# A graph-network layer on one core: GpSimd's record scatters made to wait, four by four, for the four in front

## The reference, cut to what matters

```python
h = jnp.maximum(_layernorm(x), 0.0)
xn = layernorm(h) * ln_w + ln_b
w_phys = (silu(rbf @ w1 + b1) @ w2 + b2) * cutoff[:, None]      # one row of 256 per edge
msg_phys = xn[col] * w_phys
scores = sum(Q[row] * K[col]) / sqrt(HD) * cutoff               # 8 heads
combined = msg_phys + gate * softmax(scores) * V[col]
aggr = segment_sum(combined, row, num_segments=n)
out = x + h + aggr @ wo + bo
```

## Time and profile before

| what | us |
|---|---|
| median of 3 runs | 5735.35 (5733.4 to 5738.21) |
| profiled execution, first to last instruction (its span) | 6164.1 |
| of it before the first scatter of filter rows starts | 157.8 |
| first scatter to the end of the last | 2841.3 |
| barrier, then `edges` from | 3003.07 |
| `finish`, its products from | 6049.9 to the end at 6164.1 |

### The profile page before, as it was taken

One profiled execution on the slowest core, in us unless ns is written; L12 is line 12 of the kernel. 1 busy time (PEld: TensorE's weight loads), 2 busy tenths in 40 slices (PEclk: granted clock), 3 DMA queues, 4 the chain that ended last, 5 costly groups with the idle time before them and its releaser, 6 DMA issues. The chain is left out here.

```text
span 6164.1 us, 116650 instructions
## 1 busy us (share of the span) xinstructions
PE 5392.7 (87%) x24352; PEld 3865.5 (63%) x24353; DVE 4459.1 (72%) x7861; ACT 3179.5 (52%) x10634; POOL 3908.3 (63%) x3475
## 2 busy tenths in 40 slices
PE   3778988888888988988589999999999999999999
PEld 3555655555555655655466666666666666666667
DVE  8888866555544444422389999899899999999995
ACT  4445555455555545544355555555555555555553
POOL 1666766666666666656567776667676777776671
PEclk9999999999999999999799999999999999999999
DMA  5233334333334434333599999999999999999965
GB/s 182 92 111 131 114 136 136 116 133 134 119 130 138 138 105 144 132 105 131 199 307 299 307 304 302 304 303 303 300 306 303 305 305 304 301 305 302 309 209 173
DMA packets 584375, 1306.07 MB, mean 212 GB/s; under 512 B 81230, under 2 KB 384118, under 8 KB 582945
## 3 DMA queue, kind: packets, MB, share of 16 engines
q0 software_dynamic: 221536, 881.08, 41.0%
q1 hardware_dynamic: 311780, 345.48, 18.7%
q10 hardware_dynamic: 50850, 77.03, 3.5%
HBM read 1024.15 MB, written 324.38 MB: 219 GB/s over the span
## 5 line engine op out<-in xcount | busy, mean ns | idle before, releaser
L1023 POOL DMA_INDIRECT ukvx<-kvx_table,udst x1760 | 2096.2, 1191 | 936.9 <-issue 503.1
L337 POOL DMA_INDIRECT records<-rows,slot_i x1660 | 1744.8, 1051 | 1096.8 <-ACT rows L825 589.0
L692 PE MATMUL w_ps<-w2s,hid 128*128 128x256 f32 x6656 | 1617.8, 397 | 196.1 <-DVE rows L606 167.3
L692 PEld LDWEIGHTS w_ps<-w2s,hid 128*128 128x128 f32 x6656 | 1277.6, 197 | 564.7 <-issue 210.3
L606 DVE TENSOR_TENSOR rows<-w_ps,b2b 128x512 f32<-128x512 f32 x832 | 569.4, 687 | 1104.3 <-PE w_ps L692 607.5
L806 ACT ACTIVATE hid<-hid_ps,b1t 128x512 f32<-128x512 f32 x832 | 525.4, 682 | 1227.6 <-remote 523.3
L1132 PE MATMUL ag_ps<-ukvx,uonehot 128*128 128x256 f32 x3520 | 1006.6, 405 | 155.8 <-issue 76.6
L1112 PE MATMUL uq_ps<-aggr,uonehotT 128*128 x3520 | 975.4, 400 | 1.8 <-issue 1.8
L1135 PE MATMUL ag_ps<-ukvx,uonehot 128*128 128x256 f32 x3520 | 904.2, 379 | 0.3 <-DVE ukvx L1237 0.3
L1132 PEld LDWEIGHTS ag_ps<-ukvx,uonehot 128*128 128x128 f32 x3520 | 590.1, 190 | 404.9 <-issue 313.5
L1044 ACT ACTIVATE uonehotT<-turn_ps 128x256 f32<-128x256 bf16 x880 | 328.9, 374 | 985.1 <-PE turn_ps L1104 673.5
(11 more groups left out here) (173 smaller groups left out, 4803.1 us busy)
## 6 DMA issues: line engine op xcount, KB each, us to landing
urec<-records SPq DMA_DIRECT2D x880, 260.0 KB
rbf_in<-in_edge_attr SPq DMA_DIRECT2D x207, 256.0 KB
kvx_table<-kvx ACTq DMA_DIRECT2D x10, 3456.0 KB
ukvx<-kvx_table,udst POOLq DMA_INDIRECT x1760
records<-rows,slot_i POOLq DMA_INDIRECT x1661
records<-kvx SPq DMA_DIRECT2D x1, 13000.0 KB
fbase<-x_plus_h SPq DMA_DIRECT2D x14, 896.0 KB, 7.2
out<-fout SPq DMA_DIRECT2D x13, 896.0 KB, 4.9
```

Source lines behind the costliest of these rows:

```text
L337: pool.indirect_dma_start(recs, bass.IndirectOffsetOnAxis(ap=slot_i[:, q, t:t + 1], axis=0), rows[:, q, t, :], None).then_inc(scattered[q] ...
L692: m = pe.matmul(w_ps[j % 2][:, h, :], hid[:, k % 2, c, h, j * P:(j + 1) * P], w2s[:, c, :], start=(h == 0 and c == 0), stop=(c == 1), skip ...
L1023: pool.indirect_dma_start(kvx[:, k, j, :], None, table, bass.IndirectOffsetOnAxis(ap=dst_i[:, k, j:j + 1], axis=0), bounds_check=NPAD - 1, ...
```

## The change

Ahead of every four scatters POOL now first waits until the four in front of them, in the same group or in the group before, have landed. For the second half of a group that is `scattered[q]` at this turn's start value and 64 (four DMAs of 16); for the first half it is the semaphore of the ring's place before at its full turn value. Only the very first four have nothing to wait for. The old wait on `scaled` follows behind it. Everything else stays: number, size and order of the scatters, the ring, the waits of the other engines. The tail scatter of 4 rows has no wait for a landing.

```diff
+            def landed(i, lo, k, half):
+
+                turn = i * (BODY // RING) + k // RING
+                if half:
+                    pool.wait_ge(scattered[k % RING], turn * (16 * GC) + 16 * (GC // 2))
+                elif k % RING:
+                    pool.wait_ge(scattered[k % RING - 1], turn * (16 * GC) + 16 * GC)
+                elif not (lo == 0 and k == 0):
+                    pool.wait_ge(scattered[RING - 1], turn * (16 * GC))
+
-            def scatter(g, k):
+            def scatter(i, lo, g, k):
 
                 q = k % RING
                 tail = isinstance(g, int) and g == LASTG
                 for t in range(LASTC if tail else GC):
                     if t % 4 == 0:
+                        landed(i, lo, k, t // 4)
                         pool.wait_ge(s["scaled"], g * 2 + t // 4 + 1)
                         pool.sem_inc(s["scaled_seen"], 1)
...
-                    scatter(i * BODY + k, k)
+                    scatter(i, lo, i * BODY + k, k)
```

## The result

The changed kernel takes 6641.76 us (median of 4 runs, 6638.91 to 6647.28) against 5736.78 of the kernel before: 905 us more, ratio 1.158 with a 95% interval of 1.157 to 1.160. I had 6101 and at most 6360. The direction was right and so was the bound, but the predicted loss of 366 us was less than half of the real one.

A forecast was written before the change was run, and what follows sets the result against it. PE and hand-overs paced the ranking stage; POOL would become the bound: 4.07 + 2.2 + 0.82 + 0.1 + 0.3 = 7.49 us a four, 3118 us with powers, 3009 in a run against 2643, so 6101 us, range 5868 to 6360.

The forecast's parts named there:

- the waits fit in: Rival, chance 0.05: POOL's new waits fit into its slack, a four takes 6.69 us, time within a few us of 5735.
- the change does nothing: Rival, chance 0.02: POOL's new waits are already met when reached, so the time stays 5735 us.
- fewer scatters under way speed something up: Rival, chance 0.03: at most four scatters under way let loads and landings come sooner on the DMA engines, 5615 us.
- Much slower: Rival, chance 0.15: later landings make POOL's four 7.9 to 8.2 us, the time 6316 us, or 6433 with no shortening.
- From the profile to the runs: Step for the ranking stage: every stage gives its 7% share of 429 us excess, so 2841 us becomes 2643 in a run.
- The same step, its second half: POOL's new ranking-stage time shrinks by half of the 7%, from 3118 to 3009 us in a run.
- the restart: POOL's time from landing to the next scatter's start: 0.82 us, plus 0.1 for a second wait instruction.
- The sum for a four: POOL's time per four scatters in the ranking stage: 7.49 us against 6.85 now, 3108 us for 415 fours.
- the landing: Time from the start of a four's last scatter to its landing: 2.2 us, plus 0.3 for late landings.
- The first three scatters with their gaps: POOL's time for three scatters of a four with their issue gaps, by the mean: 4.07 us.
- the predicted 10 us for the powers: POOL's 22 powers mostly run while the landing is out: at most 42 us uncovered, 10 us added to the stage.
- The slack: POOL's waiting for ACT's scaled rows in the ranking stage, 589 us or 1.42 us a four, would absorb part of the addition.

The follow-up runs named there:

- e3: The kernel before, with POOL waiting ahead of a group for the landing of the group before the last one: 5729.52 against 5735.53 us, ratio 0.9995.
- e1: The kernel before, unchanged, profiled again: run 5738.45 us, profiled span 5736.3 us.
- e5: The kernel before with the edges stage replaced by a fill of aggr with zeros: 2735.6 us in one run.
- e8: The changed kernel without the edges stage, each scatter with 64 of its 128 rows: 3484.72 us in one run.
- e9: The changed kernel, but each wait is for the four before the one in front: 5750.57 us against 5735.96 of the kernel before, ratio 1.0025.

## Why the prediction was right in kind and wrong in size

**Right.** POOL became the bound of the ranking stage; its first scatter of nearly every four waits for a landing (402 of 414); the wait for ACT has gone from 215.8 to 50.0 us, 41.7 of it ahead of the first scatter; DVE and ACT wait for the ring; the powers hide behind the landing; the edges stage didn't move. The rivals that the waits fit in, that the change does nothing, and that fewer scatters under way speed something up are out by the result and e3. The rival "Much slower", with a chance of 0.15, had the four of 8.05 us and the stage of 3341 us as they were measured; its total of 6316 to 6433 us stayed too low for the reasons under 1 and 2.

**Wrong, and where the 542 us between 366 and 908 went:**

1. *The step "From the profile to the runs".* I spread the 429 us of excess over all stages and took 2643 us for the ranking stage of the kernel before in a run. e1 has 2431.7, and e5 2429.4. That is 211 us. The prediction said that no view tells where the excess is, and held 327 us possible in the edges stage; it was 16 there. I know of no row of the first profile that would have told the stage. It was 7% long and told no landing, and to spread its excess evenly was an assumption for which no row spoke.
2. *The same step, its second half.* I let POOL's new time shrink by 3.5%, 109 us, from 3118 to 3009. The terms of POOL's time did not shrink: its scatter has a mean of 1051 ns in the disturbed profile and in e1, and the restart of 0.82 us is 0.86 with the second wait in it. A bound made of such terms doesn't scale with the execution that they were read in.
3. *The sum for a four*, 7.49 us, 3118 in all, against the measured 3340.2 / 415 = 8.05: 222 us. The mis-sized term is the landing, 2.95 us on average against 2.2 + 0.3, or 188 of the 222 us. About half of that is the median, 2.45 and not 2.2, since the semaphore comes some 0.4 us behind the last packet, which is at 2.04; the rest is late landings, 0.50 us a four and not 0.3. The first three scatters with their gaps take 4.24 us against 4.07, which is 70 us, because the mean didn't stay: first scatters became longer. The restart was right, 0.86 in all against 0.92, which gives 25 us back, and the predicted 10 us for the powers are within the measured means.
4. *The slack.* The 1.42 us a four rested on the 589 us of the disturbed profile, and 44.0 of these were ahead of the first scatter, not in the stage. In e1 the slack is (215.8 - 42.9) / 415 = 0.42 us. Before the change POOL was already in use for 93% of the stage: 1744.4 + 470.1 + 42 of 2431.7 us. This is the same error as the first, seen from POOL, and adds nothing to the 542.

The Trainium skill, page "DMA: Bandwidth & Descriptors", section "Anatomy of one DMA — SWDGE (gpsimd) path", has the rule from which the estimate of 2.3 us for the landing was worked out, nearer to the measured median of 2.4 than my 2.2. It also says that the fixed part lies mostly in the confirmation of the write. That the fixed part outweighs the bytes e8 bears out, with 2.3 against 2.4 us for half the bytes; where the fixed part lies no run here shows. The section "Latency and other measured facts" of that page would have landings get shorter when the load gets lighter; no run here shows it: the share of the DMA engines fell from 0.43 to 0.31 and the median landing stayed at 2.4 us (e1's trace tells a quarter of its landings).

None of the versions tried beats the kernel before; e3 equals it.

## What to carry to other kernels

A wait on a DMA's landing costs only when it is waited out, and then it costs landing and restart together less one ordinary step to the next scatter and less the slack, 2.0 to 2.2 us here; put at least a landing's time of other issue of the same engine between a DMA and the wait for it (e9: the waits one four later cost nothing in the stage, where they had cost 908 us). Add the price per turn to the busy time and issue gaps of that engine and compare the sum with the pace of the stage: a ring of buffers hides single late turns, never a mean that is too long. Before a trace is used for a baseline, compare its span with the runs. Where it is 7% longer, as here, no stage of it is a baseline; profile the kernel again, and don't spread the excess by a rule.

## What the runs showed that I had not expected

- One profiled execution was 7% longer than all the runs, with 410 of 428 us of excess in one stage, steps of many semaphores missing from its trace, and no engine's work longer by as much: PE's filter products 1611.7 against 1549.1 us in the ranking stage, DVE's and ACT's rows the same.
- GpSimd's scatter of 128 rows of 1,040 bytes lands 2.4 us after its start in the median, in e1 as in the changed kernel, and 2.3 us with 64 rows. The packets of the one scatter that could be read alone were through after 2.04 us; the rest is until the semaphore.
- Single landings take up to 8.5 us in the changed kernel. Over half of the lateness, 116 of 211 us, lies in the 42 fours that meet transfers of ACT's queue, and cutting 45 MB of its stores took only 14 us off the time.
- Scatters that start beside DVE's scan take 1.40 us instead of 0.97, and the first of a four is the one that meets it most often.
